# Where the last two gates are kept, and the order of work at four joints of an attention and FFN kernel

## The reference

```
s:  q, k, v = xn Wq', xn Wk', xn Wv'; q, k rotated (RoPE); causal softmax(q k' / 16) v
g:  two layers, each
      h = shift_token(g); q, k, v = split(h Wqkv), 8 heads of 64; l2norm(q) * qs; l2norm(k) * ks; xpos rotation
      local attention: blocks of 128 queries see their own block and the one before, masked; o
      g = g + o Wo
      h = layernorm(shift_token(g)) * lg + lb
      a, gate = split(h W1 + b1), 682 columns each; g = g + (a * gelu(gate)) W2 + b2
out = x + s * silu(g)
```

## Time and profile before

| | |
|---|---|
| three timed runs, median | 1438.1 us (1437.72 to 1442.6) |
| profiled execution, its own time | 1437.28 us |
| its span, first to last instruction | 1435.5 us |
| outside the span | 1.78 us |
| mean granted TensorE clock | 0.992 |
| busy: PE, DVE, ACT, POOL | 1375.0, 954.1, 880.5, 777.7 us |
| passes 1 to 4 / pass 5, 6, 7 | about 22.5 / 23.2, 22.8, 24.1 us each |
| steps 1 to 15 | 74.5 us each, 75.6 in steps 8 and 9 |

### The profile page before, as it was taken

How to read it: one execution, slowest core, us unless ns; L and a number is a source line. 1 busy time by engine, 2 the same in 40 slices (tenths; PEclk the granted TensorE clock), 3 DMA queues, 4 the chain that set the end, 5 groups by cost and what they waited for, 6 DMA issues and landing times.

```text
span 1435.5 us, 24116 instructions
## 1 busy us (share of the span) xinstructions
PE 1375.0 (96%) x7740; PEld 1048.0 (73%) x7740; DVE 954.1 (66%) x2656; ACT 880.5 (61%) x2224; POOL 777.7 (54%) x537
## 2 busy tenths in 40 slices
PE   6999997999999999999999999999999999999987
PEld 5777775777777777777777767677777777777766
DVE  5767657756666666666666777675757676766657
ACT  3555646575757574747576676656575757575764
POOL 2424757473738382837374746556564747373810
PEclk8999999999999999999999999999999999999999
DMA  7011200000000000000001010000000000000036
GB/s 217 30 58 48 66 30 1 0 1 0 0 0 0 0 0 0 0 0 0 0 2 57 4 60 1 1 0 0 0 0 0 0 0 0 0 0 0 0 126 226
DMA packets 35243, 33.33 MB, mean 23 GB/s; under 512 B 8364, under 2 KB 32896, under 8 KB 35200
## 3 DMA queue, kind: packets, MB, share of 16 engines
q1 hardware_dynamic: 35200, 32.79, 7.2%
HBM read 24.39 MB, written 8.39 MB: 23 GB/s over the span
## 4 chain that ended last, share of the span: by engine, by line
PE 77%; ACT 7%; issue 6%; DVE 5%; POOL 3%; DMA 0%; ACTq 0%; SPq 0%; POOLq 0%; DVEq 0%
PE l_psF L1375 9%; PE l_psP L829 9%; PE l_ring L829 8%; PE l_ring L1375 8%; PE l_ring L1445 7%; PE l_psP L1429 7%; PE l_psF L1463 6%; PE l_psS L1386 5%; ACT l_att L1056 4%; PE l_psS L1398 4%; PE l_psF L1415 4%; PE l_ring L1386 2%; PE l_psS L1415 2%; PE l_ring L645 2%; PE l_psS L663 1%
## 5 line engine op out<-in xcount | busy, mean ns | idle before, releaser
L938 POOL TENSOR_TENSOR l_att<-l_att 128x1024 f32<-128x1024 f32 x64 | 153.0, 2402 | 318.4 <-DVE l_att L867 318.4
L990 POOL TENSOR_TENSOR l_att<-l_att,l_rinv 128x1024 f32<-128x1024 f32 x64 | 121.2, 1893 | 67.9 <-DVE l_rinv L1223 67.9
L1036 ACT ACTIVATE l_att<-l_psP 128x384 f32<-128x384 f32 (+1 forms) x128 | 70.1, 548 | 122.8 <-PE l_psP L1429 122.8
L954 POOL TENSOR_TENSOR l_u_lo<-l_att,l_u_hi 128x512 fp32r<-128x512 f32 x90 | 115.0, 1288 | 49.1 <-ACT l_u_hi L1031 49.0
L1228 DVE COPY l_att<-l_psP 128x384 f32<-128x384 f32 (+1 forms) x128 | 78.9, 617 | 83.4 <-PE l_psP L1429 82.1
L1429 PE MATMUL l_psP<-ident,l_att 128*128 128x128 f32 x896 | 124.2, 279 | 2.1 <-DVE l_att L1228 1.5
L1429 PEld LDWEIGHTS l_psP<-ident,l_att 128*128 128x128 f32 x896 | 98.2, 141 | 32.6 <-issue 30.5
L945 POOL TENSOR_TENSOR l_att<-l_att,l_rn 128x1024 f32<-128x1024 f32 x64 | 120.8, 1909 | 0.7 <-ACT l_rn L848 0.5
L1056 ACT ACTIVATE l_att<-l_psF,l_nb 128x256 f32<-128x256 f32 x256 | 117.6, 482 | 0.0
L1216 DVE CUSTOM_DVE_ANT_0 l_psF<-l_psF,w_mask 128x256 f32<-128x256 f32 x256 | 101.2, 457 | 24.2 <-issue 24.2
L1445 PE MATMUL l_ring<-l_att 128*64 128x256 f32 (+1 forms) x1024 | 111.0, 359 | 2.0 <-ACT l_att L1036 1.4
(11 more groups left out here) (201 smaller groups left out, 4024.1 us busy)
## 6 DMA issues: line engine op xcount, KB each, us to landing
a_tables<-in_x SPq DMA_DIRECT2D x8, 512.0 KB, 4.3
scratch_s<-a_o SPq DMA_DIRECT2D x8, 512.0 KB, 3.2
l_att<-in_x SPq DMA_DIRECT2D x8, 512.0 KB, 8.4
l_att<-scratch_s SPq DMA_DIRECT2D x8, 512.0 KB, 8.9
out_dram<-l_att SPq DMA_DIRECT2D x7, 512.0 KB, 7.7
aw_stage<-in_wqkv SPq DMA_DIRECT2D x2, 768.0 KB, 5.7
l_att<-in_wqkv SPq DMA_DIRECT2D x2, 768.0 KB, 5.2
w_w_raw<-in_w SPq DMA_DIRECT2D x2, 640.0 KB
```

The lines of the kernel that those rows point to most:

```text
L938: pool.tensor_tensor(rot[:, t, :], rot[:, t, :], t2[t % 2], ALU.add).then_inc(S["added"], 1)
L954: pool.tensor_tensor(U_lo[0:rows, j, :], gate_of(j, attn)[0:rows, :], U_hi[0:rows, j, :].bitcast(F32), ALU.subtract).then_inc(S["u_lo"], 1)
L990: pool.tensor_tensor(pr, pr, along(inv, 2 * P), ALU.mult).then_inc(S["p_done"], 1)
```

## The change

Four edits, in one diff:

1. **Layers, steps 1 to 15.** Gates 4 and 5 get a place of their own in rot[:, 3], the last rotated tile, which PE has transposed by then. Unit 1's exponentials no longer wait for low halves. ACT's `u_high` of gate 5 moves from in front of `softmax(0)` to behind `softmax(1)`; the low half of gate 5 moves from POOL to DVE, behind `inverse_sum(1)` and in front of `least_of(3)`, with a semaphore of its own (`u_lo_last`).
2. **Passes.** In passes with both halves DVE does `inverse(i, 3)` and `p_copy(i, 3)` between the product and the addition of `rotate(i, 1)`, and no longer after the addition.
3. **Joint.** In pass 8 PE does `p_transposes(i, 3)` before the third part of the first projection. `values(i, 3)` writes the bank psS[0] and no longer waits for `out(i, 2)`. `project(0, 1)` waits for 31 outputs in place of 32; the 32nd is waited for before the first transposes.
4. **First step (step 0).** The transposed tiles use psS and psF in turn. The scores of unit 0, which need the first three tiles alone, come before the transposes of the last tile on PE; `least_of(0)` comes before the last `k_evac` on DVE, and `softmax(0)` before the last `q_evac` on ACT. The preloading of the table falls away in this step.

```diff
-        def out(i, t):
+        def out(i, t, bank=psO):
...
-                out(i, 3)
+                out(i, 3, psO if front else psS[0])
...
-        def rotate(i, t):
+        def rotate(i, t, between=None):
...
+            if between:
+                between()
             ge(dve, S["t1_done"], TT * i + t + 1)
             ge(dve, S["t2_done"], 2 * (TT * i + t + 1))
...
+            def last_tile():
+                inverse(i, 3)
+                p_copy(i, 3)
+            if front:
+                rotate(i, 1, last_tile if back else None)
             else:
                 first_rotation(dve, 0)
-            if back:
-                inverse(i, 3)
-                p_copy(i, 3)
+                last_tile()
...
-        def values(i, t):
+        def values(i, t, bank=psO):
...
-            if t:
+            if t and bank is psO:
                 ge(pe, S["o_sb"], TT * (i - 1) + t)
...
+            if back:
+                p_transposes(i, 3)
+            if not front:
                 first_projection(pe, 2)
             if back:
-                p_transposes(i, 3)
                 values(i, 2)
...
-                values(i, 3)
+                values(i, 3, psO if front else psS[0])
...
-    between_units = [probs[:, a, c * N:(c + 1) * N] for a in (1, 0) for c in range(2)]
+    between_units = [place[:, c * N:(c + 1) * N] for place in (probs[:, 1], probs[:, 0], rot[:, TT - 1]) for c in range(2)]
+
+    def low_done(u, j):
+        return (S["u_lo"], HFULL * u + j + 1) if j < HFULL else (S["u_lo_last"], u + 1)
...
-        return between_units[j % 4] if attn else at_end[:, j % 4, :]
+        return between_units[j] if attn else at_end[:, j % 4, :]
...
+    def turned_of(t, attn_alone):
+        return psF if attn_alone and t % 2 else psS
...
             if attn and ffn:
-                for j in range(HT):
+                for j in range(HFULL):
                     u_low(i, j, attn)
...
-            if j >= 4:
-                ge(act, S["u_lo"], HT * u + j - 3)
+            if j >= 4 and not attn:
+                ge(act, *low_done(u, j - 4))
...
-            if ffn and u < 2:
-                ge(act, S["u_lo"], HT * (i - 1) + 2 * u + 4)
+            if ffn and u == 0:
+                ge(act, *low_done(i - 1, 3))
...
+                if not ffn and j == TT - 1:
+                    softmax(i, 0, ffn)
                 if attn and 0 < j < TT:
-                    q_evac(i, j)
+                    q_evac(i, j, not ffn)
...
             if attn:
-                act.preload_act_table_set(NLE)
                 if ffn:
-                    u_high(i, HT - 1, attn)
+                    act.preload_act_table_set(NLE)
                 for u in range(UNITS + 5):
                     if 3 <= u < UNITS + 3:
                         p_evac(i, u - 3)
-                    if u < UNITS:
+                    if u < UNITS and (ffn or u):
                         softmax(i, u, ffn)
+                    if u == 1 and ffn:
+                        u_high(i, HT - 1, attn)
...
             for j in range(HT):
+                if not ffn and j == TT - 1:
+                    least_of(i, 0)
                 if attn and j < TT:
-                    k_evac(i, j)
+                    k_evac(i, j, not ffn)
...
-                    if u < UNITS:
+                    if u < UNITS and (ffn or u):
                         least_of(i, u)
                     if 1 <= u <= UNITS:
                         inverse_sum(i, u - 1)
+                    if u == 2 and ffn:
+                        u_low(i, HT - 1, attn)
...
             if attn and not ffn:
-                pe.wait_ge(C.a_out, TT * B)
+                pe.wait_ge(C.a_out, TT * B - 1)
...
+                if not ffn and j == TT - 1:
+                    scores(i, 0, TT - 1)
+                if not ffn and j == 0:
+                    pe.wait_ge(C.a_out, TT * B)
                 if attn and j < TT:
-                    transposes(i, j)
+                    transposes(i, j, not ffn)
...
-            if attn:
+            if attn and ffn:
                 scores(i, 0)
-                if ffn:
-                    ge(pe, S["u_done"], HT * (i - 1) + HFULL)
+                ge(pe, S["u_done"], HT * (i - 1) + HFULL)
                 scores(i, 1)
+            elif attn:
+                scores(i, 1, TT)
```

More of the change, by code:

```diff
@@ L1010, in high, with q_evac @@
             act.activation(hhi[:, :, :], h_view(xT, b), ACT.Copy).then_inc(S["h_hi"], 1)
-        def q_evac(i, t):
+        def q_evac(i, t, alone=False):
             ge(act, S["qT_ps"], TT * i + t + 1)
-            act.activation(QT[:, :, t * P:(t + 1) * P], psS[:, 0:512].rearrange("p (a c) -> p a c", c=P), ACT.Copy).then_inc(S["qT_sb"], 1)
+            act.activation(QT[:, :, t * P:(t + 1) * P], turned_of(t, alone)[:, 0:512].rearrange("p (a c) -> p a c", c=P), ACT.Copy).then_inc(S["qT_sb"], 1)
         def gelu(i, j, l, attn):
@@ L1130, in step @@
                 copy_v(act, i, 3)
-                q_evac(i, 0)
+                q_evac(i, 0, not ffn)
                 inverse_norm(act, i, 3)
@@ L1388, in down, with transposes, scores @@
                 last.then_inc(S["w2_ps"], 1)
[L1390 to L1392 removed]
+        def transposes(i, t, alone=False):
+            n, free_after = TT * i + t, 2 if alone else 1
             for j, (there, free, done) in enumerate((("rot_done", "qT_sb", "qT_ps"), ("rot_done", "kT_sb", "kT_ps"))):
                 ge(pe, S[there], n + 1)
[L1395 to L1396 removed]
+                if t >= free_after:
+                    ge(pe, S[free], n + 1 - free_after)
                 for a in range(INNER // P):
[L1398 removed]
+                    last = pe.transpose(turned_of(t, alone)[:, j * 512 + a * P:j * 512 + (a + 1) * P],
                                         rot[:, t, j * INNER + a * P:j * INNER + (a + 1) * P], ident[:, :])
                 last.then_inc(S[done], 1)
[L1402 removed]
+        def scores(i, u, tiles=0):
             pair, half = u // 2, u % 2
[L1404 to L1406 removed]
+            if u == 0 or tiles:
+                ge(pe, S["qT_sb"], TT * i + (tiles or TT))
+                ge(pe, S["kT_sb"], TT * i + (tiles or TT))
             if u >= 2:
```

27 lines of the change are left out of this document (8 added, 19 removed).

## The result

The changed kernel takes 1428.74 us (median of 6 runs, 1426.81 to 1429.46), the kernel before 1439.0 (6 runs on the same chip, 1437.72 to 1442.6). The ratio is 0.9925 with a 95% interval of 0.9914 to 0.9936: faster by 0.75%. Forecast were 1428 and 0.7%, with a range of 1423 to 1433.

The account below looks back on a forecast made before the run. PE was taken to bound the kernel, so only its standing still could give time back. 5.2 + 2.8 + 0 + 1.6 + 0.4 = 10.0 us off 1437.28 gives 1427.3, plus 0.8 for the median: 1428 us, range 1423 to 1433.

Parts of the forecast that it names:

- Layers: Steps 1 to 15: earlier exponentials of unit 0 give 0.35 a step (bounds 0.15 and 0.47), 5.2 us in all.
- Rival (a): Layers: the high half only changes sides in ACT's chain, 0 to 2 us gained there; 1431 to 1433 us, chance 0.22.
- The subtraction at nothing: Layers: DVE's subtraction of gate 5's low half, 0.69 long, just fits before unit 3's masking; price taken: nothing.
- (b): Layers: DVE's subtraction falls behind POOL's scaling and waits for it; PE loses about 0.9 a step, 1447 us, chance 0.07.
- The ACT page's rule: Layers: a table switch costs 2.66 us, so the edit would give nothing and the total be some 5 us less.
- Passes: Passes 1 to 4 lose the stall before values(3), 0.7 each, 2.8 us; passes 5 to 7 give nothing.
- it just fits: Passes: the last rotation ends at 74.03, and PE, 0.72 ahead, wants its transposes at 74.01 or slightly later.
- rival (d): The passes do not move because the last rotation catches PE; their 2.8 becomes 1 or less, 1430 us, chance 0.05.
- Joint: Joint: PE's waits at values(3) and project(1) both vanish, 1.6 us (bounds 1.2 and 1.7).
- First step: Step 0: unit 3's scores 1.96 earlier including the joint's 1.6, so 0.4 us for the edit (bounds -0.6 and 2.0).
- The expected fall of the clock: First step: PE's granted clock falls again as before; its absence gains 1.5 us more, an earlier fall loses 1 us.
- Rival (c): The clock stays up in the first step and the layers reach 0.47 a step: 1424.6 us, chance 0.11.

Follow-up runs that it names:

- place_only: Changed kernel, layers keeping only the place of gates 4 and 5; high half again before unit 0's exponentials, low half on POOL: 1435.47 us, ratio 0.9973.
- low_on_pool: Changed kernel with the low half of gate 5 left on POOL, between its scalings of units 0 and 1: 1430.55 us, ratio 0.9937.
- passes_alone: Kernel before with only the passes' edit (tile 3's inverse and copy between product and addition of tile 1's rotation): 1437.9 us, ratio 0.9986.
- joint_alone: Kernel before with only the joint's edit (values(3) in its own bank, earlier tile 3 transposes, later wait for the last output): 1436.62 us, ratio 0.9980.
- behind_scaling: Changed kernel with a 512-column clearing on DVE ahead of the subtraction, meant to let POOL's scaling start first: 1434.72 us, ratio 0.9969.
- second_pt_filled: Changed kernel with a second place for pair 1's transposed probabilities and 26 extra, unused PE transposes in the first step: 1422.53 us, ratio 0.9874.
- changed_again: The changed kernel itself, nothing altered, profiled once more: one execution, 1426.87 us.

## Why the prediction was right, point by point

**Layers**, 5.2 predicted (0.35 a step), 6.37 measured (0.42). The mechanism is as told. From the start of unit 0's scores (525.89 before, 522.84 after) to those of unit 2 it was 5.18 and is 4.70: 0.48 against the 0.47 worked out. To unit 4's it was 8.87 and is 8.45: 0.42 against 0.35, inside its bounds of 0.15 and 0.47. The mis-sized term is this second one. Unit 2's exponentials gained 0.25 (6.93 and 6.68 behind unit 0's scores), within the 0.15 to 0.30 of the prediction, the high half costing 0.52 from start to start. What PE did not have to wait for before was put at some 0.15 and then half left out; it gave 0.17, for unit 4's scores now start 0.05 behind the end of those exponentials (531.01 + 0.23 = 531.24; 531.29). The step was 74.2 in the prediction and is 74.11. Rival (a), that the order only moves ACT's work about, fell: steps of 74.54 come back when the order goes back (place_only).

**The subtraction at nothing** was right: 529.84 for 0.65, 0.16 ahead of POOL, the margin as worked out. The sum left out that POOL's scaling would be stretched in turn, by 0.36; it cost PE nothing, since the steps of low_on_pool, where it is not stretched, are as long. What the prediction did not see is that POOL would have had room for it as well (low_on_pool), so that this part of the edit takes on the danger of (b) and brings nothing. The SBUF page's rule (the Trainium skill, SBUF — State Buffer, "Who interferes with whom"), that a DVE instruction with two SBUF inputs and a POOL instruction that reads SBUF block each other, whoever is first, agrees with both profiles: POOL 2.25 in place of 1.89 when DVE is first, DVE 1.61 in place of 0.62 when POOL is.

**Rival (b)** did not happen, but it is real: built on purpose it gives 1448.8, where the prediction priced it at 1447. It took 1.3 a step from the changed kernel; the prediction's 0.9 lost and 0.35 not gained make 1.25. That the two are so near is in part luck: the prediction let PE lose at the scores behind unit 3's exponentials, and the trace shows the loss at the low half (0.27) and at DVE's copy (0.77).

**The ACT page's rule** (the Trainium skill, ScalarE: Activation LUTs, "What ACT_TABLE_LOAD costs") of 2.66 us for a switch would have left this edit without effect. The exponentials begin 1.30 behind the load's start, 0.02 behind its end; the measurement decides against it here.

**Passes**, 2.8 predicted, 2.3 measured: passes 1 to 4 shorter by 0.57 each in passes_alone, 5 to 7 by nothing, as predicted. The stall of 0.7 in front of values(3) is gone in all (the rows of PE's waits for DVE's copy L563 fall from 3.6 to 0.2), and the last rotation ends when it did. The step that was off is "it just fits". values(3) starts 0.70 earlier in the pass (16.04 and 15.34 behind its start), but the last transposes only 0.65 earlier (20.60 and 19.95), since they now wait for the end of the addition, and the product behind them follows 0.05 later than it did (0.41 in place of 0.36). This leaves 0.6 of the 0.7. It is rival (d) with a slack of 0.6 in place of under 0.1. In passes 5 and 7 the wait moved to the last transposes. PE's waits, before and after:

```profile
PE l_psF L654 <- DVE a_rot L547: 5.9, 4, 2.9
...
PE l_psP L680 <- DVE a_pt L561: 3.6, 7, 0.9
```
```profile
PE l_psF L657 <- DVE a_rot L549: 8.4, 4, 3.6
...
PE l_psP L683 <- DVE a_pt L563: 0.2, 1, 0.2
```

**Joint**, 1.6 predicted, 1.7 measured (0.8 and 0.9); the upper bound was right.

**First step**, 0.4 predicted, some 0.2 measured at unit 3's scores, ahead of the falls. These scores were to come 2.0 earlier, and come 1.9 earlier: 28.08 behind the last values before, 27.00 after, which is 1.1, and the joint's other 0.8 lies in front of them. 0.9 of the 1.1 is the joint's, so the edit's own part is 0.2. The mechanism is as told: unit 1's scores do stand behind the last tile's copy. Two terms are each 0.1 short: from unit 0's scores to unit 1's 4.01 where the working has 3.9, from there to unit 3's 4.07 where it has 4.0. For the whole stretch the effect can't be told from nothing, and the bounds of -0.6 and 2.0 are not contradicted. The expected fall of the clock came in most profiles, in the changed kernel's first one twice. Rival (c), no fall and 0.47 a step, gave 1424.6; the profiles have 0.42 a step, and of the three without a fall in the first step two had one in the passes; joint_alone alone had none.

**The sum**: 6.4 + 2.3 + 1.7 + 0.2 = 10.6 against 10.0 predicted and 10.3 between the medians. That it came so near is in part luck: layers were 1.2 too low, and against this passes were 0.5 and the first step 0.2 too high. The pair of profiles shows only 8.2: pass 1 began 1.4 later, in code that no edit touches, and the first step had two falls for one.

## To carry to other kernels

When one engine bounds, the order in a neighbour's queue counts by what PE waits for and not by the neighbour's busy time: 0.6 us moved behind the exponentials that release PE gave 0.42 a step for no work saved, and the next stall found in the same way gave 0.44 more. Move two-operand SBUF work from POOL to DVE only when POOL lacks the room: here it bought nothing, and one masking later in DVE's queue it cost 1.3 us a step. Where an instruction waits for several things, compare the ends of all of them before the wait is put down to one: in behind_scaling POOL was late by 0.86, and PE waited for DVE's copy. Before two profiles are subtracted, cut both into stretches and see which of them repeat in code that was not changed; here the start and the stretch with the falling clock move by 1 to 3 us on their own, as much as three of the four edits are worth.

## What the runs showed of the hardware

A clearing of SBUF on DVE (one output, no input, 128x512, 0.48) holds up POOL's instruction on SBUF just as a subtraction does: with it 0.02 ahead, POOL's scaling took 2.75 in place of 1.89, in each of the 15 steps, though the clearing and the subtraction were two instructions with a boundary between them. The subtraction alone, 0.62 long and itself not stretched, can't account for 0.86 of waiting. In both cases POOL lost some 0.14 less than the time from its start to DVE's end: 0.36 of 0.49, 0.86 of 1.00.

The granted clock falls to 0.5, the lower of its two levels, for some 3.5 us or for 7, at places that change from one execution of a program to the next: at 227.5 in one profile of the changed kernel, at 233 and 250 in the other. It also fell at the end of pass 7 in low_on_pool and at the ends of passes 5 and 7 in second_pt_filled, where other profiles of the same code show full clock. Between 40 and 262 us the 14 profiles have 19 falls. In front of each PE had stood idle for 0.9 to 2.3 us; this idle time ended at most 1.5 us before the fall or lay across its start. But idle times just as long stand at full clock elsewhere: 1.43 in front of 249.05 in changed_again, where the first profile has its second fall, and all of those in joint_alone. What decides it was not found.
